# Graph network, 64 graphs: coefficients spread by DMA through DRAM instead of by matmuls, edge-MLP units made by VectorE and ScalarE alone

## The reference, cut to what matters

```
hi = x @ W1[:H];  hj = x @ W1[H:]
h  = relu(hi[:, :, None, :] + hj[:, None, :, :] + b1)      # per edge
y  = layernorm(h @ W2 + b2) * gamma + beta
out[i] = sum_j adj[i, j] * y[i, j]
```

## Time and profile before

| | |
|---|---|
| median of 3 runs | 3257.95 us (3257.77 to 3258.49) |
| span of the profiled execution | 3262.8 us |
| instructions | 75153 |
| PE busy | 3114.7 us, 12162 matmuls |
| DVE busy | 2913.6 us, 20494 |
| ACT busy | 2498.6 us, 4612 |
| POOL busy | 2330.6 us, 3529 |
| moved by DMA | 35.86 MB, mean 11 GB/s |

### The profile page before, as it was taken

One profiled execution on the slowest core, in us unless ns is written; L12 is line 12 of the kernel. 1 busy time (PEld: TensorE's weight loads), 2 busy tenths in 40 slices (PEclk: granted clock), 3 DMA queues, 4 the chain that ended last, 5 costly groups with the idle time before them and its releaser, 6 DMA issues. The chain is left out here.

```text
span 3262.8 us, 75153 instructions
## 1 busy us (share of the span) xinstructions
PE 3114.7 (95%) x12162; PEld 1224.6 (38%) x12162; DVE 2913.6 (89%) x20494; ACT 2498.6 (77%) x4612; POOL 2330.6 (71%) x3529
## 2 busy tenths in 40 slices
PE   8999999999999999999999999999999999999995
PEld 3333333333333333333333333333333333333332
DVE  5998898898988988989989889889898898898997
ACT  7777777777777777777777777777777777777773
POOL 7777677777776776777767767777677677777772
PEclk9999999999999999999999999999999999999996
DMA  1000000000000000000000000000000000000000
GB/s 27 9 13 10 10 11 10 12 10 10 12 10 10 12 9 12 11 10 12 10 10 12 9 11 11 10 12 10 10 12 10 10 11 10 12 10 10 12 10 7
DMA packets 152776, 35.86 MB, mean 11 GB/s; under 512 B 116737, under 2 KB 152449, under 8 KB 152449
## 3 DMA queue, kind: packets, MB, share of 16 engines
q1 hardware_dynamic: 152448, 33.11, 4.9%
HBM read 18.29 MB, written 4.19 MB: 7 GB/s over the span
## 5 line engine op out<-in xcount | busy, mean ns | idle before, releaser
L400 PE MATMUL y_ps<-h,w2c 128*128 128x512 f32 x4096 | 2111.0, 597 | 19.6 <-ACT h L539 19.6
L663 DVE CUSTOM_DVE_ANT_0 h<-h,cb_ps 128x128 f32<-128x128 f32 x8192 | 1878.8, 277 | 30.8 <-PE cb_ps L422 28.1
L842 POOL TENSOR_TENSOR pre<-vT,uT 128x384 f32<-128x384 f32 (+1 forms) x2048 | 1854.0, 937 | 21.6 <-ACT vT L532 10.9
L548 ACT ACTIVATE sq<-y_ps,b2c_col 128x512 f32<-128x512 f32 x2048 | 1357.9, 682 | 34.8 <-PE y_ps L400 32.4
L539 ACT ACTIVATE h<-pre 128x896 f32<-128x896 f32 x1024 | 969.2, 946 | 353.4 <-DVE h L650 336.3
L400 PEld LDWEIGHTS y_ps<-h,w2c 128*128 128x128 f32 x4096 | 722.3, 192 | 257.5 <-issue 201.4
L422 PE MATMUL cb_ps<-c_rows,pick 96*128 96x512 bf16 x2048 | 789.1, 386 | 22.3 <-DVE gT L663 16.0
L663 DVE DVE_READ_ACCUMULATOR2_ANT gT<- 128x1 f32 x8192 | 651.8, 80 | 47.9 <-issue 47.9
L650 DVE TENSOR_SCALAR h<-vT,uT 128x128 f32<-128x128 f32 x1024 | 496.6, 486 | 122.7 <-issue 121.9
L411 PE MATMUL ss_ps<-sq,sel 128*32 128x512 f32 x4096 | 545.5, 605 | 0.1
L422 PEld LDWEIGHTS cb_ps<-c_rows,pick 96*128 96x128 bf16 x2048 | 197.6, 96 | 858.3 <-DVE gT L663 521.7
(11 more groups left out here) (95 smaller groups left out, 1930.6 us busy)
## 6 DMA issues: line engine op xcount, KB each, us to landing
devs<-dev_rows SPq DMA_DIRECT2D x512, 8.0 KB
c_rows<-c_part SPq DMA_DIRECT2D x384, 16.0 KB, 1.8
x_in<-in_x_dram SPq DMA_DIRECT2D x64, 64.0 KB, 1.8
adj_c<-in_adj_dram SPq DMA_DIRECT2D x64, 64.0 KB, 1.9
c_pair<-c_row_sum SPq DMA_DIRECT2D x256, 0.2 KB, 1.7
adj_in<-in_adj_dram SPq DMA_DIRECT2D x64, 64.0 KB, 1.8
x_res<-in_x_dram SPq DMA_DIRECT2D x64, 64.0 KB, 1.9
out_dram<-x SPq DMA_DIRECT2D x64, 64.0 KB, 1.6
```

Of the source, the lines that this page charges most:

```text
L400: pe.matmul(y_ps[:, t % 2, c0:c0 + COLS], w2c[:], h[:, t, c0:c0 + COLS], start=True, stop=True).then_inc(y_done, 1)
L548: act.activation(sq[:, t % SQ_RING, c0:c0 + COLS], y_ps[:, t % 2, c0:c0 + COLS], ACT.Square, bias=b2c_col[:], scale=float(P) ** -0.5).then ...
L663: op = dve.tensor_tensor_reduce(h[:, t, cols], h[:, t, cols], cb_ps[:, block_of_duo, k * P:(k + 1) * P], 1.0, 0.0, ALU.mult, ALU.add, gT[: ...
L842: op = pool.tensor_tensor(pre[:, t % PRE_RING, c0:c0 + units * P].rearrange("p (i j) -> p i j", j=P), vT[:].rearrange("p (o j) -> p o j", ...
```

## The change

Coefficients: VectorE multiplies the adjacency by the inverse deviations and sums the row in one instruction (`coefficients`, two per graph), and keeps them as float32. SP stores them to a scratch tensor in DRAM (`store_coefficients`, 32 KB per half graph), waits for it, and reads them back with four DMAs per half, each repeating 8 KB for all 128 partitions (`spread_coefficients`, 1 MB of SBUF written per DMA). The weighted sum reads `cb` in SBUF. `broadcast`, the 16 selecting matrices of `pick`, `c_rows` and the three bfloat16 parts are gone. LAG is 15.

Hidden units: per duo VectorE makes units 0 to 3 (in two pairs) and ScalarE units 4 to 7, each from vT with the column of uT as bias. `prepare`, `pre` and the Relu of 896 columns are gone. The squares are one instruction of 1024 columns instead of two of 512.

Later layers: GpSimd runs only set-up. Its bias sums become matmuls that accumulate into the same PSUM tile (`beta0` with adjT; `ident_eps`; biases cut in three bfloat16 parts, picked by `pick`), and x_base, x1s and c_sum go to VectorE. `adj_in` itself is used until the third product of L3, so it is loaded later. The tile `small_ps` is now three banks. TAIL_SLOT is 13 and several places in AT move.

```diff
-LAG = 14
+LAG = 15
-TAIL_SLOT = 12
+TAIL_SLOT = 13
+        c_dram = nc.dram_tensor("c_scratch", (2, P * SPAN), F32, kind="Internal").ap()
+        cb = sb("cb", [P, 2 * CHUNKS, 2 * DUO_UNITS * P])
-        cb_ps = ps("cb_ps", [P, 2, COLS])
@@ sync
-            def line_up_coefficients(g, half):
...
+            def store_coefficients(g, half):
+                wait_apart(sp, c_made, 2 * g + half + 1)
+                for p in range(CHUNKS):
+                    wait_apart(sp, cb_in[CHUNKS * half + p], 16 * g)
+                wait_apart(sp, c_stored[half], 16 * g)
+                sp.dma_start(c_dram[half].rearrange("(b j) -> b j", j=SPAN), c[:, half, :]
+                             ).then_inc(c_stored[half], 16)
+            def spread_coefficients(g, half):
+                wait_apart(sp, c_stored[half], 16 * (g + 1))
+                for p in range(CHUNKS):
+                    wait_apart(sp, ttr_done, SLOTS * (g - 1) + HALF * half + 2 * p + 2)
+                    src = c_dram[half].rearrange("(q p a) -> q p a", q=4, p=CHUNKS)[:, p, :]
+                    sp.dma_start(cb[:, CHUNKS * half + p, :].rearrange("k (q a) -> k q a", q=4),
+                                 src.partition_broadcast(P)).then_inc(cb_in[CHUNKS * half + p], 16)
+            def load_tail(g):
+                wait_apart(sp, l3_agged[LAYERS - 1], g)
...
@@ tensor
-            def broadcast(g, t, block_of_duo):
...
+                    pe.matmul(prod, gT_keep[:], w2cg[:], start=True, stop=False)
+                    pe.matmul(prod, adjT[:], beta0[:], start=False, stop=True).then_inc(l0_made, 1)
...
+                        pe.matmul(prod, aggT[:], l3w[:, i, :], start=True, stop=False)
+                        pe.matmul(prod, pick[:], bias_parts[:, 1 + i, :], start=False, stop=True
+                                  ).then_inc(l3_made[i], 1)
@@ scalar
-                act.activation(h[:, t, DVE_UNITS * P:], pre[:, t % PRE_RING, :], ACT.Relu).then_inc(h_made, 1)
+            def hidden(g, t, n):
+                if n == BLOCK_UNITS:
+                    wait(act, ttr_done, SLOTS * (g - 1) + t + 1)
+                    if t == 0:
+                        wait(act, uv_ready, g + 1)
+                i = unit_of(t, n)
+                op = act.activation(h[:, t, n * P:(n + 1) * P], vT[:], ACT.Relu, bias=uT[:, i:i + 1])
+                if n == DUO_UNITS - 1:
+                    op.then_inc(h_act, 1)
+            def squares(g, t):
+                act.activation(sq[:, t % SQ_RING, :], y_ps[:, t % 2, :], ACT.Square,
                                bias=b2c_col[:], scale=float(P) ** -0.5).then_inc(sq_done, 1)
@@ vector
+                c0 = (t % 2) * DUO_UNITS * P + n * P
+                op = dve.tensor_tensor_reduce(h[:, t, cols], h[:, t, cols], cb[:, t // 2, c0:c0 + P],
                                               1.0, 0.0, ALU.mult, ALU.add, gT[:, i:i + 1])
+            def coefficients(g, half):
+                wait(dve, inv_done, 2 * g + half + 1)
+                wait(dve, adj_c_in, 16 * (g + 1))
+                wait(dve, c_stored[half], 16 * g)
                 wait(dve, c_pair_in, 64 * g)
+                dve.tensor_tensor_reduce(c[:, half, :], adj_c[:, half, :], invs[:, half, :], 1.0, 0.0,
+                                         ALU.mult, ALU.add, c_row_sum[:, half:half + 1]).then_inc(c_made, 1)
+                if due("x_base"):
+                    dve.scalar_tensor_tensor(out=x_base[:], in0=b2cg[:], scalar=c_sum[:], in1=x_res[:],
+                                             op0=ALU.mult, op1=ALU.add).then_inc(x_base_set, 1)
+                if due("x1_scaled"):
+                    dve.tensor_scalar(x1s[:], x1[:], dis[:], None, ALU.mult).then_inc(x1s_set, 1)
-                    steps = DVE_UNITS + DUO_UNITS
+                    steps = 2 + DUO_UNITS
                     for k in range(steps):
+                        if k in (1, 3):
+                            if new is not None:
+                                hidden(new, s, k - 1)
+                                hidden(new, s, k)
+                        elif wg is not None:
+                            weighted_sum(wg, t, k - (k > 1) - (k > 3))
                         later_layers(g, place0 + k * FINE // steps, place0 + (k + 1) * FINE // steps)
+                        for gg, half, at in ((old, 1, 3), (new, 0, 11)):
+                            if s == at and gg is not None:
+                                if k == 5:
+                                    invert(gg, half)
+                                if k == 6:
+                                    coefficients(gg, half)
@@ gpsimd
-            def prepare(g, t):
-            def coefficients(g, half):
-            def later_layers(g, lo, hi):
...
```

More of the change, by code:

```diff
@@ L158, in build @@
         c_sum = sb("c_sum", [P, 1])
[L159 to L162, removed]
+        x_base = sb("x_base_t", [P, P])
         z = sb("z", [P, P])
@@ L218, in build @@
             sem("l2_agged"), sem("l2_agg_kept"), sem("l2_made1"), sem("l2_relued"), sem("l2_made2"))
-        l3_based = [sem(f"l3_based{i}") for i in range(LAYERS)]
         l3_agged = [sem(f"l3_agged{i}") for i in range(LAYERS)]
@@ L450, in later_layers @@
                     wait(pe, normed["ln1"], g + 1)
-                    wait(pe, adj_self_set, g + 1)
-                    pe.matmul(prod, x2[:], adj_self[:], start=True, stop=True).then_inc(l2_agged, 1)
+                    pe.matmul(prod, x2[:], adj_in[:], start=True, stop=False)
+                    pe.matmul(prod, x2[:], ident_eps[:], start=False, stop=True).then_inc(l2_agged, 1)
                 if due("l2_mm1"):
@@ L496, in iteration @@
                     yg, t = (new, s - 1) if s >= 1 else (old, SLOTS - 1)
-                    wg, wt = (new, s - LAG) if s >= LAG else (old, s + SLOTS - LAG)
                     if s == SLOTS - 1 and after is not None:
                         make_uv(after)
-                    if wg is not None:
-                        broadcast(wg, wt, 0)
                     if yg is not None:
                         products(yg, t, 0)
-                    if wg is not None:
-                        broadcast(wg, wt, 1)
                     if s == 10 and after is not None:
@@ L597, in later_layers @@
                             wait(act, z_set["ln3"], g)
-                        else:
-                            wait(act, l3_based[i], g + 1)
                         act.activation(h3[:], z_aff[:], ACT.Relu).then_inc(l3_relued[i], 1)
@@ L617, in iteration @@
                         later_set_up()
+                    g, place0 = tail_graph(s, old, older)
+                    sg, t = (new, s - 2) if s >= 2 else (old, s + SLOTS - 2)
+                    later_layers(g, place0, place0 + FINE // 4)
+                    if sg is not None:
+                        squares(sg, t)
                     if s == 2 and old is not None:
@@ L928, in _ @@
             pool.memset(sel[:, ROWS - 1:ROWS], 1.0).then_inc(ones_set, 1)
-            pool.memset(c_rows[:], 0.0).then_inc(ones_set, 1)
+            pool.wait_ge(ones_set, 3)
+            pool.wait_ge(ident_set, 1)
+            pool.memset(bias_parts[:], 0.0).then_inc(set_up, 1)
+            pool.wait_ge(later_weights_in, 16 * LATER_WEIGHTS)
             pool.wait_ge(set_up, 1)
-            prepare(0, 0)
-            prepare(0, 1)
-            def iteration(new, after, old, older):
-                for s in range(SLOTS):
-                    if is_graph(new, 1) and s == LATER_SET_UP_SLOT:
-                        pool.wait_ge(later_weights_in, 16 * LATER_WEIGHTS)
-                        pool.wait_ge(affine_set, 2)
-                        pool.wait_ge(eps_set, 2)
-                        pool.wait_ge(mask_set, 1)
-                    g, place0 = tail_graph(s, old, older)
-                    if s == 12 and new is not None:
-                        coefficients(new, 0)
-                    if s == 4 and old is not None:
-                        coefficients(old, 1)
-                    later_layers(g, place0, place0 + FINE // 2)
-                    if s + 2 < SLOTS and new is not None:
-                        prepare(new, s + 2)
-                    if s + 1 == SLOTS and after is not None:
-                        prepare(after, 0)
-                        prepare(after, 1)
-                    later_layers(g, place0 + FINE // 2, place0 + FINE)
-            program(pool, iteration)
+            for k in range(PARTS):
+                rows = slice(32 * k, 32 * k + 32)
+                rest = bias_row if k % 2 == 0 else bias_rest
+                pool.tensor_copy(bias_parts[rows], rest[rows]).then_inc(bias_set, 1)
+                pool.wait_ge(bias_set, k + 1)
+                if k < PARTS - 1:
+                    pool.tensor_copy(bias_head[:], rest[:]).then_inc(bias_split, 1)
+                    pool.wait_ge(bias_split, 2 * k + 1)
+                    into = bias_rest if k % 2 == 0 else bias_row
```

(2 more changed lines are left out.)

314 lines of the change are left out of this document (96 added, 218 removed), and 16 rows, old and new, of the table AT.

## The result

The changed kernel takes 3852.6 us (median of 4 runs, 3851.7 to 3856.3), the kernel before beside it 3258.2 (3257.8 to 3259.2): a ratio of 1.183, 95% interval 1.181 to 1.184. The forecast was 3480 with a range to 3740. The direction was right, the size was not: 594 us lost where 222 were expected. The profiled execution's span is 3854.5 us.

What follows compares the result with a forecast made beforehand. VectorE was taken to set the period of 50.0 us a graph, TensorE 4 us behind; 50.0 - 6.2 + 9.6 - 0.3 + 0.6 + 0 - 0.2 = 53.5 us, so 3480 us, range 3350 to 3740 (8 in 10).

Steps and rivals of the forecast that it cites:

- Part 5: VectorE's stall of 2.9 us a graph at the loop's turn stays: change taken as 0, bounds -0.8 to +0.8.
- Part 6: Waits on small matmuls shorten because TensorE is freer: -0.2 us a graph, bounds -0.5 to +1.5.
- Part 3: VectorE's weighted sum reads coefficients from cb in SBUF, not cb_ps: -0.3 us a graph, bounds 0 to -1.3.
- rival B: Not slower: the weighted sum is quicker from SBUF; at 60 ns each, 2995 us; chance 6%.
- part 1: GpSimd leaves the loop, so VectorE's stretched instructions shorten: -6.2 us a graph, bounds -4.8 to -7.1.
- part 2: VectorE makes 4 units of each eight instead of 1: +9.6 us a graph, bounds +9.1 to +13.4.
- part 4: Small work moves from GpSimd to VectorE: +0.6 us a graph, bounds 0.4 to 1.0.
- Rival A: The coefficient spreads bind, since DMA reads one place repeatedly slowly: 59 us a graph, 3830 us (far case 11.8 ms); chance 18%.
- 20 us and 205 GB/s: Condition for the coefficient load staying hidden: four spreads take under 20 us, or 205 GB/s.
- Rival C: TensorE's clock falls in a stretch of two slots per turn: +3.4 us a graph, 3695 us; chance 7%.

Runs made afterwards that it cites:

- experiment 1: The changed kernel with every spread moving 128 bytes of each 2 KB piece (a sixteenth of the bytes, same number of pieces): 3636.3 us, ratio 1.115.
- experiment 8: The changed kernel with 128-byte pieces in the spreads of half 0 only, those of half 1 whole: 3647.2 us, ratio 1.120.
- experiment 4: The changed kernel with a hinted branch back at the end of each engine's loop: 3436.1 us, ratio 1.053.
- experiment 11: The changed kernel with the hinted branch and VectorE's reciprocal and coefficient product at the eighth and ninth of a slot's ten steps: 3461.6 us, ratio 1.062.
- experiment 5: The kernel before with the hinted branch alone: 3184.0 us, ratio 0.977.
- units-only kernel: The kernel before with four units of a duo by VectorE, four by ScalarE, none by GpSimd; coefficients still spread by matmuls: 3411.0 us, ratio 1.046.
- experiment 9: The kernel before with added spread-shaped DMA traffic that nothing reads (8.4 MB a graph) and the hinted branch: 3200.7 us, ratio 0.982.

## Why the prediction was wrong

The forecast of 53.5 us a graph was 49.4 of VectorE's work and 4.1 of waits. Measured were 50.6 and 9.1.

- Part 5 failed, and is the largest term of the miss, 3.0 of 6.3 us. It kept the stop at 2.9 us "since the loop is turned as often", with bounds of 0.8 for where the code lies. The stop is 5.9. I had found it, called it a stop for nothing that the profile shows, and left it at that; the row that shows its cause, the instruction queue's packets on the page, I didn't put beside it. Then an 8.39 MB stream was laid over exactly that moment: the half-0 product is made in slot 11, so its spreads are in flight at the turn. Size, from experiments 1 and 8: +3.1 us. It is not the whole miss: with the stop back at the forecast's size those two kernels still take 56.1 us a graph, above the forecast's own range of 52.0 to 55.3. The Trainium skill, "Runtime: NRT & Kernel Launch", section "Instruction fetch mechanics", says that a taken branch to code outside the loaded window forces a fetch before execution goes on; the trace agrees for the plain branch, with a stop of 2.7 us without traffic and 5.5 with it; behind the hinted branch, taken as often, it shows no fetch.
- Part 6, other waits, -0.2 with bounds to +1.5: they went from 1.4 to 3.3 us, +1.9. Two thirds of it, 1.25 us, is the wait for devs, from 0.24 to 1.5; experiments 4 and 11 divide it between the stop and the reciprocal's earlier place in the slot (it stood at the eighth of nine steps and stands at the sixth of ten). The order within a slot was in the diff, and I didn't read it as a term. The wait for cb brought 0.4 over that for cb_ps.
- Part 3, the weighted sum from SBUF: forecast -0.3, measured 0.212 us between neighbours for 0.208, +0.5. The nearest row, L752 against L769 in the earlier trace rows, had the size (4 ns) but not the sign. The rule of the Trainium skill that rival B cited ("VectorE: DVE Perf Modes", section on the TRN2 errata) would have made it an estimated 65 ns cheaper; the trace contradicts it.
- Parts 1, 2 and 4 together: forecast +4.0, measured +4.4 (45.7 to 50.6, less the 0.5 of part 3). Right: units at 0.20 us, L728 (the former L760) at 347 ns for 640, L733 at 350 for 532, the one-column product at 160 for 669. (The values taken in part 1 add up to 6.35 where it has 6.2, and its lower bounds to 4.7 for 4.8; it changes nothing.)
- Rival A, the spreads bind, named nearly the right time (3830) and is still wrong. The four spreads issued from 1034.27 us on have all landed at 1054.37, 20.1 us later: 4.19 MB at 209 GB/s, with hardly a margin over the 20 us and 205 GB/s that I asked for, and the wait for cb is 0.7 us. The transfers harmed a fetch, not their reader. Who looks at the total alone would take A as confirmed.
- Rival C, the clock: it did fall, to 0.50 in the 6 us after the stop; against it the forecast had held that the work is spread evenly, and at the turn it was not. It is a result of the stop: with the hint the mean granted clock is 0.98 for 0.93. Its price is 0.9 us a graph in z_aff's wait, which is part of why the hint gives back some 7 us where the stop was 5.9.
- The range: the upper bounds of all parts together give 50.0 - 4.8 + 13.4 + 0 + 1.0 + 0.8 + 1.5 = 61.9 us, but only by part 2's bound of 0.28 us a unit, which did not come; with the 9.6 that did they end at 58.1, below 59.8. No case had the idle time of the main engine grow for a reason outside the data.

What bounded the kernel before was read rightly as VectorE, but its lead over TensorE was 1.4 us, not 4 (experiment 5).

Without traffic the stop is 2.07 + 0.81 us in the kernel before, 2.8 in the changed one with small pieces and 1.9 in the units-only kernel, so it doesn't follow the length of the body (386, 427 and 436 instructions). The table behind experiment 9 says why: in all of them VectorE goes on 3.0 us after its branch, and what differs is how long it still has work behind the branch, 0.95, 0.16 and 1.13 us. Left open: what decides how much work it has left there, and why the body before stops a second time in a turn. Where the code lies in the fetched blocks may matter; that was not tried. Nor do the runs show why the wait for devs stays at 1.5 us with the shorter stop of experiment 1 and falls to 0.9 without any.

## What to carry over

A stop of the main engine after the loop's branch, with nothing to wait for, was here a fetch of instructions, and a price in itself: look for it beside the instruction queue's packets, ask what other transfers will be in flight at that moment, and hint the branch before anything else is tuned (here 2.3% on the old kernel, 10.8% on the new one). Moving an operand from PSUM into SBUF is not neutral while GpSimd works: a two-input VectorE instruction was stretched from 284 to 391 ns. A time that matches a rival is no proof of it; the waits view has to name the same place.

## What the hardware showed that I had not expected

- The stop at the turn takes 2.7 us beside quiet queues and 5.5 us beside spreads that hold the DMA engines 95% of the time; in the kernel before with added traffic its two pieces took 6.9 and 4.2 us. The instruction packet itself takes 0.3 to 0.5 us in either case. It starts 1.0 to 1.1 us after VectorE's branch beside quiet queues, 4.1 and 6.0 beside the transfers, and VectorE goes on 1.9 to 2.0 us after it starts.
- With the hinted branch the instruction packets fell from 318 to 22 in the whole span, and to none in the turns: a VectorE body of 427 instructions is then not fetched again.
- Four spreads of 128 x 8 KB out of one 32 KB stretch of DRAM, issued in a row, move 209 GB/s from the first issue to the last landing, where repeated 512-byte rows moved 45 GB/s.
- After the turn's stop, in which TensorE stood idle for 6.84 us, it came out at a granted clock of 0.50: the four y_ps records after it took 3.62 us, 0.9 each, where two such records took 0.86 together in the earlier trace rows. TensorE's timeline in the changed kernel:

```profile
1053.51 0.79 PE L406 MATMUL prod_bank<-adjT,x1s 128*128 128x128 f32 x2 [6.84 <-DVE x1s L700]
1054.09 3.62 PE L370 MATMUL y_ps<-h,w2c 128*128 128x512 f32 x4
```
